# Embedding lookup and FM term on one core: weight loads issued by SP in line with x, and x loads of eight tiles

## The reference

```python
embs = [jnp.dot(x, w) for x, w in zip(xs, ws)]
emb_sum = sum(embs)
q_emb = sum(jnp.dot(x ** 2, w ** 2) for x, w in zip(xs, ws))
fm_ans = 0.5 * (emb_sum ** 2 - q_emb)
return jnp.concatenate([fm_ans] + embs, axis=-1)
```

## Time and profile before

| | us |
|---|---|
| median of the runs | 277.24 |
| the profiled execution | 277.28 |
| its span (first to last instruction) | 275.5 |
| DVE busy | 222.2 (81%) |
| ACT busy | 225.6 (82%) |
| PE busy | 214.9 (78%) |
| POOL busy | 117.5 (43%) |
| DMA, mean over the span | 413 GB/s |

### The profile page before, as it was taken

The page is one execution under the profiler, slowest core; times in us unless marked ns, Lnnn a source line. Parts: engine busy times, 40 slices in busy tenths (PEclk is TensorE's granted clock), DMA queues, the critical chain, the costliest instruction groups (busy, mean ns, idle before and its releaser), DMA issues.

```text
span 275.5 us, 2719 instructions
## 1 busy us (share of the span) xinstructions
PE 214.9 (78%) x894; PEld 151.5 (55%) x894; DVE 222.2 (81%) x132; ACT 225.6 (82%) x272; POOL 117.5 (43%) x83
## 2 busy tenths in 40 slices
PE   0529889799988777878886887787688788698995
PEld 0416566576756555556664654554555555466752
DVE  2776876888798898878978978978987987999973
ACT  0648998999987788889868868868877887899984
POOL 0446667685414109257224134134045041083934
PEclk9977999999999999999999999999999999999999
DMA  7999999999999999999999999999999999999996
GB/s 257 436 412 431 419 424 414 427 425 426 421 425 425 421 426 421 422 426 427 421 432 422 426 423 424 423 426 430 418 426 428 421 431 425 407 420 415 410 396 231
DMA packets 15710, 113.92 MB, mean 413 GB/s; under 512 B 2000, under 2 KB 3280, under 8 KB 9168
## 3 DMA queue, kind: packets, MB, share of 16 engines
q1 hardware_dynamic: 11088, 106.96, 92.6%
q10 hardware_dynamic: 4608, 6.79, 6.7%
HBM read 110.85 MB, written 2.88 MB: 413 GB/s over the span
## 4 chain that ended last, share of the span: by engine, by line
DMA 71%; issue 13%; ACT 10%; PE 3%; POOLq 1%; POOL 1%; ACTq 1%; DVE 0%; SPq 0%
DMA x_ring<-in_x_dram 62%; DMA whole<-in_w_dram 8%; ACT is_set L380 7%; PE sums L518 2%; ACT turned L391 1%; ACT whole L372 1%; POOLq L197 1%; POOL is_one L498 1%; ACT results L396 1%; ACT L372 0%; ACTq L366 0%; ACT turned L440 0%; PE sums L573 0%; DVE is_one L614 0%; ACT odd_flag L443 0%
## 5 line engine op out<-in xcount | busy, mean ns | idle before, releaser
L614 DVE TENSOR_SCALAR_CACHE_REDUCE is_one<-x_ring 128x4096 uint8<-128x4096 f32 (+2 forms) x58 | 218.4, 3776 | 45.7 <-DMA x_ring<-in_x_dram 44.5
L380 ACT ACTIVATE is_set<-x_ring 128x2048 fp32r<-128x2048 uint32 (+2 forms) x106 | 190.1, 1796 | 32.1 <-DMA x_ring<-in_x_dram 31.7
L518 PE MATMUL sums<-is_set,low 128*128 128x512 f32 x396 | 133.0, 417 | 57.2 <-ACT is_set L380 42.5
L518 PE MATMUL sums<-is_set,high 128*128 128x512 f32 x396 | 125.2, 397 | 0.0
L518 PEld LDWEIGHTS sums<-is_set,low 128*128 128x128 f32 x396 | 68.3, 191 | 97.4 <-ACT is_set L380 42.7
L474 POOL CAST high<-whole 128x1024 fp32r<-128x1024 f32 (+5 forms) x31 | 27.1, 875 | 141.1 <-ACT whole L372 141.1
L518 PEld LDWEIGHTS sums<-is_set,high 128*128 128x128 f32 x396 | 75.5, 191 | 17.4
L476 POOL TENSOR_TENSOR low<-whole,high 128x1024 fp32r<-128x1024 f32 (+5 forms) x31 | 60.8, 1960 | 2.5
L372 ACT ACTIVATE whole<-whole 128x512 f32<-128x512 f32 (+5 forms) x31 | 16.5, 536 | 7.0 <-DMA whole<-in_w_dram 6.9
L380 ACT ACTIVATION_READ_ACCUMULATOR is_set<-x_ring 128x1 f32 x106 | 19.8, 186 | 0.0
L487 POOL TENSOR_TENSOR total<-total,turned 128x1024 f32<-128x1024 f32 x8 | 19.2, 2399 | 0.0
(11 more groups left out here) (38 smaller groups left out, 14.7 us busy)
## 6 DMA issues: line engine op xcount, KB each, us to landing
x_ring<-in_x_dram SPq DMA_DIRECT2D x42, 2048.0 KB, 21.3
x_ring<-in_x_dram SPq DMA_DIRECT2D x9, 1024.0 KB, 19.1
x_ring<-in_x_dram SPq DMA_DIRECT2D x11, 512.0 KB, 17.8
whole<-in_w_dram ACTq DMA_DIRECT2D x21, 256.0 KB, 9.7
out_dram<-results SPq DMA_DIRECT2D x9, 256.0 KB, 9.1
x_ring<-in_x_dram SPq DMA_DIRECT2D x4, 256.0 KB, 14.3
whole<-in_w_dram ACTq DMA_DIRECT2D x2, 192.0 KB, 7.2
whole<-in_w_dram ACTq DMA_DIRECT2D x4, 64.0 KB, 8.8
```

The costliest lines, as they stand in the source:

```text
L380: nc.scalar.activation(is_set[chunk.k % SETS][:, 0:length], in_ring(chunk.place, length).bitcast(U32), ACT.Sign, accum_out=set_counts[:, c ...
L518: last = nc.tensor.matmul(sums[:, summing(n, half), :], w, x[:, at:at + HALF], start=first, stop=False, skip_group_check=True)
L614: nc.vector.tensor_scalar(is_one[c % 2][:, 0:length], in_ring(at, length), 1.0, None, ALU.is_equal, ALU.add, accum_out=one_counts[:, c:c + ...
```

## The change

The weight loads move from ACT to SP, in line with the x loads: ahead of the first x load of group g, SP issues all weight loads up to group g + 1, each with its wait for `parts_ready`. `AHEAD` goes from 3 to 2, so that ACT squares group g + 1 (not g + 2) in group g. The x of groups 7 to 12 (table 1), 14 (table 6) and 15 to 23 (table 0) comes in loads of eight tiles, one for each group, with two counts of four tiles each. The ring grows from 20 to 24 tiles; the masks go from 5 to 4 buffers and the pairs of weight parts from 4 to 3.

```diff
-RING = 20
+RING = 24
+
+JOINED = {1: 6, 6: 1, 0: 9}
 LANDS = 16
 
-SETS = 5
+SETS = 4
 
 WHOLES = 3
-PAIRS = 4
-AHEAD = 3
+PAIRS = 3
+
+AHEAD = 2
...
-        if len(one.halves) == 1:
+        whole = one.tile < JOINED.get(one.table, 0) * GROUP
+        if whole and one.at:
+
+            load = counts[-1].loads[0]
+            counts.append(Count(len(counts), [load], chunks))
+            counts[-1].at, counts[-1].length = load.at + LOAD * BATCH, LOAD * BATCH
+            place = counts[-1].at
+            for chunk in chunks:
+                chunk.place, place = place, place + chunk.n * chunk.width
+                chunk.load = load
+            load.count = counts[-1]
+            continue
+        if whole:
+            parts = [(one.tile, GROUP)]
+        elif len(one.halves) == 1:
             parts = [(one.tile, 1), (one.tile + 1, 1)]
...
-            free = 0
+            def load_w(group):
+                if group.g >= WHOLES:
+
+                    sp.wait_ge(parts_ready, group.g - WHOLES + 1)
+                at, n = group.tile * D, group.tiles
+                sp.dma_start(whole[group.whole][:, 0, 0:n, :], w_dram[group.table][:, at:at + n * D]
+                             ).then_inc(w_landed[group.whole], 16)
+
+            free, fetched = 0, 1
             for load in LOADS:
+                if load.i == 1:
+                    load_w(GROUPS[0])
+                while load.i > 0 and fetched < min(load.group.g + AHEAD, NGROUPS):
+                    load_w(GROUPS[fetched])
+                    fetched += 1
                 if load.free > free:
...
-            for group in GROUPS[:AHEAD]:
-                load_w(group)
             act.wait_ge(constants, 8)
             for group in GROUPS[:AHEAD - 1]:
                 square(group)
             for group in GROUPS:
                 for c, chunk in enumerate(group.chunks):
                     count_set(chunk)
-                    if c == min(1, len(group.chunks) - 1):
-                        if group.g + AHEAD < NGROUPS:
-                            load_w(GROUPS[group.g + AHEAD])
                     if c == min(2, len(group.chunks) - 1) and group.g + AHEAD - 1 < NGROUPS:
                         square(GROUPS[group.g + AHEAD - 1])
```

More of the change, by code:

```diff
@@ L159, in plan_counts @@
         counts.append(Count(len(counts), own, chunks))
+        if whole:
+            counts[-1].length = LOAD * BATCH
         place = own[0].at
@@ L165, in plan_counts @@
         for load in own:
-            load.count = counts[-1]
+            load.count, load.group = counts[-1], one.group
         loads += own
@@ L360, in _ @@
         def _(act):
[L361 to L367, removed]
             def square(group):
```

## The result

The changed kernel takes 283.87 us (median of 6 runs, 282.99 to 285.44) against 277.24 before, a ratio of 1.0244 with a 95% interval of 1.0223 to 1.0265. It is slower, as forecast, but by 6.6 us and not by 2.8, and outside the range of 278.4 to 282.4. The profiled execution took 284.25 us, its span is 282.5.

The account below looks back on a forecast made before the run. The DMA stream was taken as the bound: 277.28 + 3.5 (start) - 1.2 (rows) + 0.2 (ring) + 0.2 (weights 8) = 279.98, so 280.0 us, with a range of 278.4 to 282.4.

Parts of the forecast that it names:

- Where the ring is short: Waits around groups 14, 16 and 17 leave little x in flight: +0.2 us for all, at worst +1.8.
- weights 8: SP's wait for group 5's parts, the tightest early wait, covered by 0.7 to 1.5 us: priced +0.2, between 0 and +1.5.
- What bounds the kernel: The DMA stream bounds the time; after the last x lands some 8.5 us of small work follow.
- The hole at the start: SP waits for group 0's parts until 9.2 us, engines dry at 7.15: +3.5 us, between 3.05 and 3.9.
- the restart: After a wait ends, engines need 1.0 us (first byte) to 1.84 us (full-rate equivalent) from issue.
- Rival (c): Ring with two large loads in flight opens true holes at groups 14, 16, 17: +3 us more, 283.0 us; chance 0.10.
- The range: 278.4 to 282.4 us: from start 3.05 with saving 1.9, to start 3.9, no saving and 1.2 of other holes.
- Larger rows: Loads of eight tiles mean 128 fewer packets per engine, at 8 to 15 ns each: -1.2 us.
- Rival (b): Start's hole exists but large rows save 3.0 to 4.0 us, at 432 to 435 GB/s: 277.0 to 278.0 us; chance 0.07.
- Weights in line: Weight packets on SP's queue in line with x, not beside it, neither gain nor cost: 0.
- Squares, masks, pairs: In the steady part, squaring one group ahead, four masks and three pairs of weight parts cost nothing: 0.

Follow-up runs that it names:

- e10: Weights on SP behind x, aligned loads of eight, with three more groups of table 0 in loads of eight (twelve, not nine): 279.89 us, ratio 1.0093 to the kernel before.
- e4: The kernel before with only the weight loads moved to SP and AHEAD = 2; ring of 20 and loads of four kept: 282.25 us, ratio 1.0196.
- e6: The changed kernel with SP's starting order mended: x 2 and 3 issued ahead of weights 3, weights 0 to 2 still early: 279.98 us, ratio 1.0112.
- e5: The changed kernel with weights issued by ACT again and loads of eight at ring places 0, 8 and 16 alone: 276.91 us, ratio 0.9986.
- e8: The changed kernel with weights issued by ACT again and no loads of eight tiles, at most four: 277.18 us, ratio 1.0000.
- e7: The changed kernel with weights still on SP but behind x in its list, and loads of eight at ring places 0, 8, 16: 276.52 us, ratio 0.9984.
- e9: The changed kernel with the mended starting order and loads of eight at ring places 0, 8 and 16 alone: 277.91 us, ratio 1.0035.

## Why the prediction was wrong

The direction, the bound and the largest single term were right; the size was not. The step that failed is "Where the ring is short": its three holes, at the wait for weights 15 and at the ring's waits for x of groups 16 and 17, were put at +0.2 us together and cost 3.2 us by the rates and 3.5 by the medians, which have weights 8 in them. Walked back by medians, the loss of 6.6 us is: start 283.87 - 279.98 = 3.9, ring 279.98 - 277.91 = 2.1, the wait for weights 15 (with that for weights 8) 277.91 - 276.52 = 1.4, and what is left is 0.7 below the kernel before. By the intervals of the ratios each of the first three is uncertain by some 0.7 us. The rates of the changed kernel's own trace, which owe nothing to the experiments, give 3.9, 1.6 (95 to 115 us) and 1.6 (115 to 145).

- **What bounds the kernel**: right. In every kernel but e10 the span ends 8.4 to 8.7 us behind the last x.
- **The hole at the start**: right in place and cause (e4, e6). SP was released at 8.91 us where I took 9.2, and the engines were dry by 7.0 and not at 7.15, as 7.00 x 248 = 1.74 MB is all that they moved where I had 1.91. It cost 3.9 us against 3.5, the upper end of its bounds, and with 0.7 of uncertainty the two can't be told apart. The engines are not only idle: up to 11.0 us they come back at 38, then 304, then 248 GB/s. Of the two ends for the restart, that of the first start (1.84 us from the issue to full rate) was the better one.
- **Where the ring is short**: this is the step that failed. I put three places at +0.2 us together, at worst +1.8; they cost 2.1 for the ring and most of 1.4 for weights 15. Rival (c) had such holes and 283.0 us, at a chance of 0.10, though its condition, that the issue comes more than 9.8 us behind the landing, did not hold. The issue of weights 15 was timed right: x of group 11 landed at 94.25 us, and they went out at 104.19, T + 9.9. What was wrong is when the engines run dry. I let all 16 end a load together, 0.8 us ahead of its landing. In the trace the landing is the moment of the last of them: for x of group 11, of group 12 and of the one tile the first engine is 2.5 to 2.6 us ahead of it and the mean engine 1.7 to 1.8. Up to 14.3 us first and last engine are 0.3 to 0.5 us apart for x; the spread then grew, to 0.8 us at 20 us and 2.5 from 53 us on. The kernel before has up to 2.8 us of it too, at no cost while more is on order. Why the engines drift apart stays open.
- The ring's own waits came late as well. x of groups 16 and 17 went out at 126.26 and 137.74 us, 9.2 us behind the landings at 117.06 and 128.53 and not 8.75. I took DVE's 8.7 us as the longer pass; but after a table's end ACT also copies its sums, 1.0 us among these masks, which makes its 8.1 us 9.1, and SP's waits for the ring are for ACT (18.9 us).
- The restart was the third part of it. The first packet of an engine behind a hole is slow: of the 2048 packets of 32 KB, 1213 ns in the median, 57 took over 1400 ns, and 42 of these, up to 2207 ns, start within 0.5 us of 105.9, 127.2 and 138.6 us, right behind the three holes. So a hole costs up to 1 us beside its idle time.
- **The range** took 1.2 us for all other holes, where my own bounds were 1.8 for the ring and 1.5 for weights 8; with these its upper end would have been 284.5 and not 282.4.
- **Larger rows**: mis-sized. I took -1.2 us; e5 against e8 gives -0.27 and e7 against e8 -0.66. The rate from 145 to 240 us is 426 GB/s in the changed kernel where I had 426 to 428, but only 424, the rate of before, in e5 and e7, which have the same loads. The line through the small rows of the tail seems to overstate what a packet costs beside its bytes; by how much is not settled, as e5 has a low stretch of 0.8 us of its own. The Trainium skill's 3 cycles per packet ("Why small descriptors are slow", DMA: Bandwidth & Descriptors), -0.45 us by my estimate, lies between the two measured values. Rival (b) falls, since the full stream stays at 426 GB/s.
- **Weights in line**: 0 was right. e7 has them in line, e5 beside x, 276.52 and 276.91, with intervals that overlap.
- **Squares, masks, pairs**: 0 was right (e8).
- **Weights 8**: the wait was named with a cover of 0.7 to 1.5 us and priced at 0.2. It costs 0.2 us in the profiled execution of the changed kernel (30 to 60 us at 419 GB/s against 422 before), 0.9 in that of e4 and 2.0 in that of e9. Its mean price was not measured by itself, and part of the 1.4 us above is its.

The sum by the measured terms, 277.28 + 3.9 + 2.1 + 1.4 - 0.7 = 284.0, matches the result, but not as an independent check, since the terms are differences of a chain that ends in it. The rates above are one. By independent pairs the ring is 279.33 - 276.91 = 2.4, and the rows are 0.27, so 0.4 us of the 0.7 are without a cause of their own; e7's interval is wide enough for that.

## What to carry to other kernels

When the DMA stream is the bound, a semaphore wait on the issuing engine is priced by what is on order behind it. The bare sum of the bytes on order is not enough for that price: here the first engines were dry 2.5 us ahead of a landing, and the first packets behind a hole took up to 1 us more. One large load more on order than the sum asks for covers both: e7 waits behind the x ahead of which the changed kernel waits, and has no such hole. In a ring, check at each wrap how many loads stay in flight, and let large loads start at multiples of their size; one odd tile ahead of them cost 2 us here. Late large loads delay the consumer even without a hole (e10), so the last loads should stay small.

## What the runs showed of the hardware

Two things I had not expected. The 16 steps of one load's semaphore spread as the stream goes on, from 0.3 us at the start to 2.5 us at 100 us (101.51 to 104.06 for a load of 4 MB, 103.44 to 105.94 for the 512 KB behind it), and fall back to 0.8 us behind a hole (106.28 to 107.05 for weights 15). With little queued behind, the first engines then stand idle while the last still work. And the first packets of 32 KB behind a hole take up to 2207 ns, against 1213 in the median.
